# A decoder layer on one Trainium2 core: key loads and table stores in pieces of 32 rows, first phase and rounds resequenced

## Chip, cores and metric

The kernel runs on one core of one Trainium2 chip. The metric is the device time of one execution in microseconds (us). The engines are TensorE (PE), VectorE (DVE), ScalarE (ACT), GpSimd (POOL) and SyncE (SP, which here only issues DMAs).

## What is computed

```python
x = x + swat(layernorm(x))                    # windowed sigmoid attention
x = x + wkv(w, u, k=layernorm(x), v=ctx)      # a recurrence over the 256 rows
x = x + ffn(layernorm(x))                     # ternary weights, 8-bit activations
# swat: 16 heads of 32; K and V are one head of 32 for all
K = rope(x @ wk.T) @ k_compress.T @ k_decompress.T;  V = (x @ wv.T) @ v_compress.T @ v_decompress.T
K, V = quant_dequant_8bit(K), quant_dequant_8bit(V)      # min and max over the whole tensor
for i in range(0, s, 64):                                # windows of 128, step 64
    a = sigmoid(Q[i:i+128] @ K[i:i+128].T * scale);  a = a / (a.sum(-1) + 1e-8)
    out[i:i+128] = blend(out, a @ V[i:i+128])            # linear ramp over the overlap
# ffn, every linear with round(w / mean|w|) in -1, 0, 1 and rows of x on an 8-bit grid
h = silu(x @ gate.T) * (x @ up.T);  h = rms_norm(h) * ln_weight;  x = x + h @ down.T
```

x is 16 batches of 256 rows by 512, float32; gate and up are 2048 x 512, down is 512 x 2048. K and V need the minimum and maximum over all batches, and a weight's grid needs the mean of the whole weight.

## The kernel before

Each engine has a program of its own, written out by hand (`sync_program`, `tensor_program`, `scalar_program`, `vector_program`, `pool_program`); an engine runs its program in order and waits on semaphores (class of events: `x.at(i)` is the count after step i). What runs when is thus set by these five lists and by nothing else. The DMA queue is SP's for nearly all transfers, ACT's for the stores of raw keys and values; a DMA issue also takes its place in the issuing engine's order.

**First phase** (to 78.88 us). For each of 8 pairs of batches, SP loads x (`load_x`, L265) and its transpose (`load_columns`, L271), PE projects keys and values (`keys_project`, L441), spreads the row statistics (L454) and, one pair later, takes the low-rank step (`keys_grow`, L463, L470); DVE makes the statistics, the rope (L917, L924) and the minima and maxima (`keys_ext`); ACT copies the raw keys and values out of PSUM and stores them to DRAM scratch (`keep_raw`, L682 to L690). SP stores, two pairs later still, the cosine and sine rows with the row scaling to the same scratch (`store_trig`, L279). wq is centred with column means from PE (L478) and one pass on DVE (`queries_centre`, L910). DVE sets the grid after an all-reduce on POOL. Of the 12 weight chunks of 1 MB (three weights GATE, UP, DOWN of four chunks) SP loads one at a time into a buffer (`load_weights`, L288), ACT sums the absolute values (`sum_weights`, L698), POOL and DVE make the mean of four chunks (`weight_mean`, L972 to L977), and DVE rounds each chunk (`round_weights`, L936, L939, L945: three passes). The buffer is free for a next chunk when the chunk has been rounded.

**Rounds** i = 0 to 18. Round i has attention of batch b = i, the recurrence of w = i - 1, gate and up of f = i - 2, down of g = i - 3 and the output of h = i - 4. In a round:

- PE: `queries` (L508, two halves), `wkv_keys` (L569, transposes), `gate_up(f, t, k)` (L597; t row half, k column quarter), `scores(b, c)` (L527, four groups of four heads), `down(g, t, k)` (L607), `dens` and `nums` (L538, L541), `wkv_back` (L578), `attention_out` (L559).
- ACT: `set_keys` (L717, L719, L723: the windows of K and V from the loaded rows and the grid), `silu` (L786), `squares` (L791, with the sum of a row), `exps` (L777), `probs` (L734), `logs` and `inverses` (L741, L746), `wkv_logs` and `wkv_inverses` (L752, L757), `scale_tokens` (L764), `scale_hidden` (L770). sigmoid, exp, log and silu change the function table, a row ACT_TABLE_LOAD.
- DVE: `keys_grid` (L1023 to L1029), `blend_windows` (L1051 to L1054), `hidden` (L1160, gate times up), `hidden_scale` (L1176 to L1182), `wkv_residual` (L1110), `wkv_norm` (L1116, L1012), `peak` (L1167, L1169: the sum of the squares and the largest value of the hidden rows), `wkv_quantise` (L1017, L1126 to L1142), `residual` (L1061, L1063), `wkv_round` (L1149), `rope` (L1037), `hidden_round` (L1189), `rotate` (L1043), `values` (L1073), `scan` (L1082), `join` (L1090), `refine` (L1097), `quotient` (L1104), `output` (L1194).
- POOL: `weigh_windows` (L1347), `weigh_hidden` (L1364), statistics (L1324, L1370), `key_steps` (L1354).
- SP: `turn_queries` (L328: neighbouring rows of the rotated queries swapped, two DMAs for each half), `turn_tokens` (L336) and `turn_hidden` (L343), DMA transposes; `load_keys` (L312 keys with cosine and sine, L316 values), `load_queries` (L302), `load_values` (L321), `load_residual` (L297), `store` (L348).

The next queries need the residual rows (`residual`, L1061), which stand on DVE behind `peak` and `wkv_quantise`; `peak(g, 1)` needs the last squares of its half:

```python
            if do_g:
                peak(g, 1)
            if do_f:
                wkv_quantise(f)
            if do_w:
                residual(w)
```

The key load takes 32 rows of 3 x 256 values of a batch's scratch and writes them four times, to partitions 0 to 127; in front of each row lie three windows of the values.

Of the kernel before, what the change touches and what calls it, by code (L numbers as in the profile page):

```python
# [13 lines left out]
P = 128  # L14
# [25 lines left out]
def build(nc, a, out, k_scratch, v_scratch):  # L40
# [118 lines left out]
    v_raw = [raw[k][:, 1] for k in range(4)]  # L159
# [40 lines left out]
    kv_loaded = event("kv_loaded", 2, 16)  # L200
# [11 lines left out]
    key_grown, key_raw, key_ext = event("key_grown", 2), event("key_raw", 2), event("key_ext", 2)  # L212
    w_summed, w_round, w_bound, w_tern = [
# [46 lines left out]
    def sync_program(sy):  # L260
# [30 lines left out]
        def load_residual(b):  # L291
            if b == 0:
                sy.wait_ge(key_bn.sem, key_bn.at(PAIRS - 2))
# [10 lines left out]
        def load_keys(b):  # L304
            if b:
# [59 lines left out]

        for j in range(PAIRS):
# [6 lines left out]
        sy.dma_start(wq_sb[:, :, :], a["wqT"].rearrange("(c p) n -> p c n", p=P)).then_inc(wq_loaded.sem, 16)  # L373
        load_queries(0)
        load_keys(0)
        load_weights(GATE, 0)
        load_weights(GATE, 1)
        store_trig(5)
        load_weights(GATE, 2)
        load_weights(GATE, 3)  # L380
        store_trig(6)
        load_residual(0)
        store_trig(7)
        load_values(0)
        for i in range(B + 3):
# [4 lines left out]
            if do_g:  # L390
                turn_hidden(g, 0, 0)
            if do_b:
                turn_queries(b, 1)
            if do_g:
                turn_hidden(g, 0, 1)
            if i == 0:
                load_weights(UP, 0)
            if i == 1:
                load_weights(DOWN, 1)
            if do_g:  # L400
                turn_hidden(g, 1, 0)
            if do_b:
                next_keys(b)
            if do_g:
                turn_hidden(g, 1, 1)
# [1096 lines left out]
```

## Time and profile before

| | |
|---|---|
| Median of 3 runs | 1096.46 us (1096.4 to 1097.68) |
| The profiled execution: its time | 1100.16 us |
| its span | 1098.8 us |
| mean granted TensorE clock | 0.922 |
| PE busy | 878.8 us, 80% |
| DVE busy | 844.1 us, 77% |
| ACT busy | 706.2 us, 64% |
| POOL busy | 435.7 us, 40% |
| DMA | 106.90 MB, mean 97 GB/s |

Busy times count instructions at work; a wait on a semaphore or for a buffer is idle time. The last column group of a window gives the granted clock, the mean busy share of the 16 DMA engines and what they moved. In a timeline a row groups neighbouring instructions of one line; in brackets stands how long the engine was idle before, and what released it. Rows of SP are DMA issues: their time is that of the issue, not of the transfer. The whole span of 40 slices begins with the DMA at 328 and 314 GB/s for two slices of 27.5 us each and falls to about 80 in the rounds.

### The profile page before, as it was taken

What the parts mean: (1) busy time and instruction counts of PE and PEld (TensorE: products, weight loads), DVE (VectorE), ACT (ScalarE), POOL (GpSimd) and SP (SyncE); (2) the same over time, 40 slices, a digit from 0 to 9 for tenths busy, and PEclk for the clock granted to TensorE, in tenths of its full rate; (3) what the DMA queues carried; (4) which work ended last, traced back from release to release, by engine and by line L of the source; (5) the groups of instructions that cost most, each with busy time, mean ns of one, the idle gap of its engine ahead of it and who ended that gap; (6) DMA issues with size and microseconds to landing.
All of it is one profiled execution on the core that took longest, in us unless ns stands there. A gap on an engine that the chain in (4) does not pass through costs nothing.

```text
span 1098.8 us, 22051 instructions
## 1 busy us (share of the span) xinstructions
PE 878.8 (80%) x8388; PEld 516.9 (47%) x8388; DVE 844.1 (77%) x1630; ACT 706.2 (64%) x1179; POOL 435.7 (40%) x494
## 2 busy tenths in 40 slices
PE   5883656678888888888888888989898888886665
PEld 2342545445454555555545555555455555553222
DVE  4744477887888888888887888888877888876953
ACT  0114737276868686868777777777786868684633
POOL 2100113236263635353535453535454444444522
PEclk9986776869999999999999999999999999997878
DMA  8876424020515151515142524242424343212022
GB/s 328 314 231 246 151 100 148 19 85 10 103 59 103 55 107 54 107 51 99 63 95 67 84 78 84 78 84 79 84 78 72 91 67 95 68 59 40 28 59 67
DMA packets 125754, 106.90 MB, mean 97 GB/s; under 512 B 99312, under 2 KB 101088, under 8 KB 124496
## 3 DMA queue, kind: packets, MB, share of 16 engines
q1 hardware_dynamic: 119344, 101.47, 35.6%
q0 software_dynamic: 624, 2.59, 0.7%
q10 hardware_dynamic: 5680, 1.42, 0.6%
q8 instruction: 66, 1.08, 0.4%
q14 instruction: 40, 0.33, 0.1%
HBM read 65.62 MB, written 10.49 MB: 69 GB/s over the span
## 4 chain that ended last, share of the span: by engine, by line
ACT 30%; PE 26%; DVE 20%; issue 15%; SPq 5%; DMA 2%; POOL 2%; DVEq 0%; ACTq 0%; POOLq 0%
PE bank L508 9%; ACT arena L734 6%; PE bank L607 5%; PE bank L527 4%; ACT L786 3%; ACT sums L741 3%; DVE junk L1160 3%; PE bank L597 3%; ACT sums L746 2%; ACT junk L786 2%; ACT junk L791 2%; DVE amax L1126 2%; DVE fs L1169 2%; ACT L757 2%; ACT L734 2%
## 5 line engine op out<-in xcount | busy, mean ns | idle before, releaser
L597 PE MATMUL bank<-w_up_gate,qT 128*128 128x512 bf16 x1024 | 244.9, 389 | 40.4 <-ACT junk L786 20.6
L1364 POOL TENSOR_TENSOR work<-junk,lnw 128x512 f32<-128x512 f32 x128 | 188.3, 1491 | 126.0 <-DVE junk L1160 111.7
L1347 POOL TENSOR_TENSOR sums<-sums,blend 128x448 f32<-128x448 f32 x64 | 73.6, 1170 | 274.2 <-ACT sums L746 274.2
L597 PEld LDWEIGHTS bank<-w_up_gate,qT 128*128 128x128 bf16 x1024 | 97.2, 100 | 155.8 <-ACT junk L786 26.3
L508 PE MATMUL bank<-wide,wq_sb 128*128 128x256 f32 x512 | 120.8, 397 | 34.8 <-DVE rows L1061 30.8
L607 PE MATMUL bank<-w_down,work 128*128 128x512 bf16 x512 | 132.0, 408 | 19.8 <-ACT junk L786 10.5
L508 PEld LDWEIGHTS bank<-wide,wq_sb 128*128 128x128 f32 x512 | 100.6, 199 | 61.2 <-issue 46.9
L734 ACT ACTIVATE arena<-bank 128x384 f32<-128x384 f32 x256 | 104.9, 497 | 36.0 <-PE bank L527 35.8
L527 PE MATMUL bank<-wide,k_win 32*128 32x128 f32 x1536 | 69.7, 317 | 72.9 <-ACT arena L734 54.2
L786 ACT ACTIVATE junk<-bank,deq 128x512 f32<-128x512 f32 x128 | 86.3, 686 | 54.0 <-PE bank L597 52.2
L559 PE MATMUL bank<-wo_sb,wide 128*128 128x512 f32 x256 | 115.8, 607 | 2.6 <-DVE wide L1054 2.6
L1160 DVE TENSOR_TENSOR junk<-bank,junk 128x512 f32<-128x512 f32 x128 | 87.6, 685 | 29.1 <-PE bank L597 15.8
L527 PEld LDWEIGHTS bank<-wide,k_win 32*128 32x128 f32 x1536 | 56.1, 211 | 97.1 <-ACT arena L734 71.9
L770 ACT ACTIVATE work<-work,fs 128x2048 f32<-128x2048 f32 x32 | 63.9, 1996 | 58.5 <-DVE fs L1182 58.5
L1082 DVE TENSOR_TENSOR_SCAN sums<-wkv_s,sums 128x256 f32<-128x256 f32 x128 | 98.6, 838 | 0.0
L791 ACT ACTIVATE junk<-junk 128x512 f32<-128x512 f32 x128 | 80.7, 630 | 20.7 <-DVE junk L1160 20.6
L607 PEld LDWEIGHTS bank<-w_down,work 128*128 128x128 bf16 x512 | 48.0, 103 | 87.0 <-issue 23.1
L559 PEld LDWEIGHTS bank<-wo_sb,wide 128*128 128x128 f32 x256 | 49.8, 195 | 60.5 <-issue 55.6
L1037 DVE TENSOR_TENSOR wide<-bank,kv_b 128x512 f32<-128x512 f32 x64 | 41.0, 682 | 45.7 <-PE bank L569 38.6
L1169 DVE TENSOR_REDUCE fs<-work 128x1 f32<-128x2048 f32 x32 | 72.8, 2276 | 0.4 <-POOL work L1364 0.4
L764 ACT ACTIVATE wide<-wide,amax 128x512 f32<-128x512 f32 x32 | 21.4, 714 | 79.2 <-DVE amax L1138 79.2
L538 PE MATMUL bank<-arena,v_win 128*32 128x128 f32 x1536 | 57.7, 285 | 9.9 <-ACT sums L741 8.1
(150 smaller groups left out, 1536.9 us busy)
## 6 DMA issues: line engine op xcount, KB each, us to landing
sums<-in_xT SPq DMA_DIRECT2D x8, 1024.0 KB, 11.2
wide<-in_xT SPq DMA_DIRECT2D x16, 512.0 KB, 3.8
rows<-in_x SPq DMA_DIRECT2D x16, 512.0 KB, 4.9
ctx_T<-in_ctxT SPq DMA_DIRECT2D x16, 512.0 KB, 3.7
wide<-wide SPq DMA_DIRECT2D x64, 128.0 KB, 2.0
out<-rows SPq DMA_DIRECT2D x32, 256.0 KB, 2.1
kv_b<-k_raw SPq DMA_DIRECT2D x16, 384.0 KB
work<-in_wgT SPq DMA_DIRECT2D x4, 1024.0 KB, 16.4
```

The lines of the kernel that those rows point to most:

```text
L508: last = te.matmul(in_bank(k, 2)[:, n % 2, :], wq_sb[:, c, n * P:(n + 1) * P], xT[:, c, :], start=c == 0, stop=c == NC - 1)
L527: last = te.matmul(bank[j][:, n * P:(n + 1) * P], k_win[head, window], q_cos[head, c, window], start=True, stop=True, skip_group_check=True)
L559: last = te.matmul(bank[t][:, :], heads_T[:, c, t * P:(t + 1) * P], wo_sb[:, c, :], start=c == 0, stop=c == NC - 1)
L597: last = te.matmul(bank[4 + k % 4][:, :], qT[:, c, t * P:(t + 1) * P], w_up_gate[:, m, c, cols], start=c == 0, stop=c == NC - 1)
L607: last = te.matmul(bank[6 + t][:, :], hid_T[:, t, c, :], w_down[:, c, :], start=c == 0, stop=c == NI - 1)
L734: se.activation(prob[:, :, QUAD * c + j, :], bank[j][:, 0:NW * P].rearrange("p (k q) -> p k q", k=NW), ACT.Sigmoid, scale=float(1.0 / np.s ...
L786: se.activation(gated[:, n % 2, :], bank[4 + 2 * (n % 2)][:, :], ACT.Silu, scale=deq[:, 0, t:t + 1]).then_inc(silu_set.sem, 1)
L791: se.activation(gated[:, n % 2, :], hid[:, n % 2, :], ACT.Square, accum_out=fs[:, t, n:n + 1]).then_inc(sq_set.sem, 1)
L1082: ve.tensor_tensor_scan(state[:, c, n, 1:S + 1], sc["decay"][:, c:c + 1].to_broadcast([P, S]), GG[:, c, n, :], 0.0, ALU.mult, ALU.add).the ...
L1160: ve.tensor_tensor(hid[:, n % 2, :], bank[4 + k % 4][:, :], gated[:, n % 2, :], op=ALU.mult).then_inc(hid_set.sem, 1)
L1169: ve.tensor_reduce(col[t]["am"], hid_w[:, t, :], AX.X, ALU.max, apply_absolute_value=True).then_inc(h_peak.sem, 1)
L1364: ge.tensor_tensor(hid_w[:, t, cols], hid[:, n % 2, :], lnw[:, cols], op=ALU.mult).then_inc(z_set.sem, 1)
```

## The change

- `load_keys` writes the keys in four DMAs of 32 rows in place of one that repeats its source four times; the values come from a scratch laid out as they are used (128 rows of 96 values), for which ACT copies the windows in order before it stores them (three more copies a pair, into space that is free at that time).
- `store_trig` still issues two DMAs, each now of 32 rows by 2 by 256 in place of 2 by 32 by 256.
- wkvT is laid out contiguous and loaded by SP, with low_rank, ahead of everything; SP no longer waits for the two before the second pair; the transpose of x is loaded ahead of x.
- wq and the first queries' rows are loaded after pair 5; wq's means are taken a pair earlier, and its centring stands before the last pair's minima and maxima. ACT issues the loads of the first residual and context.
- Loads, sums and roundings of the weights stand at other places of rounds 0 to 2.
- In every round all five engines' lists are in another order.

```diff
         for j in range(PAIRS):
+            load_columns(j)
             load_x(j)
-            load_columns(j)
-            if j == 0:
-                sy.wait_ge(first_loads.sem, first_loads.at(0))
             if j >= 3:
                 store_trig(j - 3)
...
-            for u in both:
-                sy.dma_start(k_scratch[2 * j + u, :, S:].rearrange("e (n s) -> n e s", n=2),
-                             rope_rows[j][0:2 * HD, u, :]).then_inc(trig_stored[j % 4].sem, 16)
+            for n in both:
+                sy.dma_start(k_scratch[2 * j:2 * j + 2, :, (n + 1) * S:(n + 2) * S].rearrange("u e s -> e u s"),
+                             rope_rows[j][n * HD:(n + 1) * HD]).then_inc(trig_stored[j % 4].sem, 16)
...
-            sy.dma_start(kv_b[:, NW * HD:], k_scratch[b].unsqueeze(0).to_broadcast([QUAD, HD, 3 * S])).then_inc(
-                kv_loaded.sem, 16)
-
-            windows = bass.AP(v_scratch.tensor, v_scratch[b].offset, [[HD, P], [BLK * HD, NW], [1, HD]])
-            sy.dma_start(v_q, windows).then_inc(kv_loaded.sem, 16)
+
+            for k in range(QUAD):
+                sy.dma_start(kv_b[k * HD:(k + 1) * HD, NW * HD:], k_scratch[b]).then_inc(kv_loaded.sem, 16)
+            sy.dma_start(v_q, v_scratch[pair, :, b % 2]).then_inc(kv_loaded.sem, 16)
...
+            new = bank[TOK_BANK[j % 2]][:, 0:4 * 2 * HD].rearrange("p (u t g e) -> p g u t e", u=2, t=NT, g=2)[:, 1]
+            se.copy(v_rows[j % 4][:, :, 0:NW:2, :], new).then_inc(val_rows.sem, 1)
+            se.copy(v_rows[j % 4][0:BLK, :, 1, :], new[BLK:P, :, 0, :]).then_inc(val_rows.sem, 1)
+            se.copy(v_rows[j % 4][BLK:P, :, 1, :], new[0:BLK, :, 1, :]).then_inc(val_rows.sem, 1)
...
-            if j == PAIRS - 1:
+            if j == PAIRS - 2:
                 te.wait_ge(wq_loaded.sem, wq_loaded.at(0))
                 column_means(bank[0][:, :], wq_sb, wq_mean)
...
+            if j == PAIRS - 1:
+                queries_centre()
...
             if do_g:
                 turn_hidden(g, 0, 0)
+                turn_hidden(g, 0, 1)
+                turn_hidden(g, 1, 1)
             if do_b:
                 turn_queries(b, 1)
-            if do_g:
-                turn_hidden(g, 0, 1)
-            if i == 0:
-                load_weights(UP, 0)
+            if i == 0:
+                load_weights(GATE, 3)
...
+            if do_w:
+                values(w)
+                scan(w, 0)
             if i == 2:
                 round_weights(DOWN, 3)
+            if do_b:
+                rotate(b, 1)
```

(The line numbers of the changed kernel are a few higher: L288 is L292 there, L328 is L329, L791 is L795, L1043 is L1048.)

SP's queue from the last table store of the pairs' loop to round 0. Before:

```order
L279 DMA k_raw<-w_down 2x32x256 x2
L373 DMA wq_sb<-in_wqT 128x4x512
L302 DMA wide<-in_xT 128x1024
L312 DMA kv_b<-k_raw 128x1x768
L316 DMA kv_b<-v_raw 128x3x32
L288 DMA work<-in_wgT 128x2048 x2
L279 DMA k_raw<-w_down 2x32x256 x2
L288 DMA work<-in_wgT 128x2048 x2
L279 DMA k_raw<-w_down 2x32x256 x2
L297 DMA rows<-in_x 128x1024
L279 DMA k_raw<-w_down 2x32x256 x2
L321 DMA ctx_T<-in_ctxT 128x1024
L328 DMA wide<-wide 64x512 x4
```

and now:

```order
L283 DMA k_raw<-w_down 32x2x256 x2
L316 DMA kv_b<-k_raw 32x768 x4
L317 DMA kv_b<-v_raw 128x96
L292 DMA work<-in_wgT 128x2048
L283 DMA k_raw<-w_down 32x2x256 x2
L292 DMA work<-in_wgT 128x2048
L283 DMA k_raw<-w_down 32x2x256 x4
L292 DMA work<-in_wgT 128x2048
L329 DMA wide<-wide 64x512 x4
L292 DMA work<-in_wgT 128x2048
L292 DMA work<-in_wuT 128x2048 x2
```

The swaps (L328, now L329) stood behind four GATE chunks, the residual's and the context's loads; now three chunks are ahead of them and the fourth is behind.

ACT at the boundary of two full rounds, from the last silu of one round to the exps of the next (fs is the sum of squares and the scales, v_win and k_win are what `set_keys` writes). Before:

```order
L786 ACTIVATE junk<-bank,deq 128x512
L791 ACTIVATE junk,fs<-junk 128x512 x2
L770 ACTIVATE work<-work,fs 128x2048
L764 ACTIVATE wide<-wide,amax 128x512 x2
L717 ACTIVATE v_win<-kv_b,grid 128x96
L719 ACTIVATE v_win<-kv_b,grid 64x32
L723 ACTIVATE k_win<-kv_b,grid 128x256
L770 ACTIVATE work<-work,fs 128x2048
L786 ACTIVATE junk<-bank,deq 128x512
L777 ACT_TABLE_LOAD
L777 ACTIVATE sums<-bank,wkv_s 128x256 x4
```

and now:

```order
L795 ACTIVATE junk,fs<-junk 128x512
L721 ACTIVATE v_win<-kv_b,grid 128x96
L723 ACTIVATE v_win<-kv_b,grid 64x32
L727 ACTIVATE k_win<-kv_b,grid 128x256
L795 ACTIVATE junk,fs<-junk 128x512
L774 ACTIVATE work<-work,fs 128x2048
L768 ACTIVATE wide<-wide,amax 128x512 x2
L774 ACTIVATE work<-work,fs 128x2048
L790 ACTIVATE junk<-bank,deq 128x512
L795 ACTIVATE junk,fs<-junk 128x512
L790 ACTIVATE junk<-bank,deq 128x512
L781 ACT_TABLE_LOAD
```

`set_keys` has moved from behind `scale_tokens` to ahead of the last squares, and the first squares and a second silu stand ahead of the exps.

## Rows read from the trace of the kernel before

**Rows 1.** Windows: us, busy us (instructions) by engine, TensorE clock, DMA share, GB/s
```profile
0.00:78.88 78.88, 59.19 (x197) 27.46 (x197) 43.96 (x127) 9.15 (x19) 12.75 (x25) 0.97 0.87 295
78.88:141.77 62.89, 35.68 (x400) 26.36 (x401) 30.97 (x53) 34.30 (x48) 6.65 (x8) 0.68 0.54 184
141.77:204.18 62.41, 34.42 (x417) 26.26 (x417) 46.38 (x81) 30.93 (x50) 13.57 (x14) 0.73 0.33 109
...
323.65:379.33 55.68, 48.37 (x512) 28.96 (x513) 46.90 (x92) 42.05 (x72) 26.07 (x29) 1.00 0.35 80
```

**Rows 2.** Waits of SP, 10 to 111 us
```profile
SPq L265 <- DMA arena<-in_low_rank: 9.5, 1, 9.5
```

**Rows 3.** SP timeline, first phase: start, duration, what [idle before, releaser]
```profile
66.20 6.71 SPq L279 DMA_DIRECT2D k_raw<-w_down  x2
...
92.44 2.48 SPq L328 DMA_DIRECT2D wide<-wide  x4
```

**Rows 4.** Timeline of PE, first phase and first scores
```profile
26.88 3.63 PE L441 MATMUL bank<-sums,arena 128*96 128x512 f32 x8
...
32.78 3.63 PE L441 MATMUL bank<-sums,arena 128*96 128x512 f32 x8
...
63.00 3.67 PE L441 MATMUL bank<-sums,arena 128*96 128x512 f32 x8 [1.09 <-DMA sums<-in_xT]
...
78.88 10.14 PE L508 MATMUL bank<-wide,wq_sb 128*128 128x256 f32 x32 [3.96 <-DVE wq_sb L910]
102.00 1.67 PE L527 MATMUL bank<-wide,k_win 32*128 32x128 f32 x24 [12.97 <-DVE wide L1043]
```

**Rows 5.** The chain that ended last, 78 to 105 us
```profile
93.00 8.13 DMA wide<-wide
```

**Rows 6.** The page's DMA issues: count, KB each, median us to landing
```profile
wide<-wide SPq DMA_DIRECT2D x64, 128.0 KB, 2.0
```

**Rows 7.** Timeline of ACT, end of round 0
```profile
130.62 1.91 ACT L698 ACTIVATE junk<-work 128x2048 f32<-128x2048 f32 x1
```

**Rows 8.** Timeline of DVE, end of round 0
```profile
136.83 0.15 DVE L974 TENSOR_SCALAR w_mean<-abs_tot 128x1 f32<-128x1 f32 x1 [4.02 <-POOL abs_tot L1328]
...
140.94 0.68 DVE L1061 TENSOR_TENSOR rows<-bank,rows 128x512 f32<-128x512 f32 x1
```

**Rows 9.** Two windows of the first phase (columns as above)
```profile
15.00:40.00 25.00, 25.00 (x81) 10.91 (x80) 22.11 (x66) 3.14 (x8) 6.07 (x10) 1.00 1.02 391
41.70:43.70 2.00, 2.00 (x9) 0.64 (x7) 0.74 (x2) 0.00 (x0) 0.00 (x0) 1.00 0.54 91
```

**Rows 10.** Timeline of ACT, a full round
```profile
342.19 1.64 ACT L734 ACTIVATE arena<-bank 128x384 f32<-128x384 f32 x4
...
371.66 0.63 ACT L791 ACTIVATE junk<-junk 128x512 f32<-128x512 f32 x1 [0.28 <-DVE junk L1160]
...
379.59 0.45 ACT L717 ACTIVATE v_win<-kv_b,grid 128x96 f32<-128x96 f32 x1
...
380.50 0.60 ACT L723 ACTIVATE k_win<-kv_b,grid 128x256 f32<-128x256 f32 x1
```

**Rows 11.** Timeline of DVE, the same round
```profile
373.03 0.12 DVE L1167 TENSOR_REDUCE fs<-fs 128x1 f32<-128x4 f32 x1
```

**Rows 12.** Timeline of SP's queue, the same round
```profile
335.95 1.10 SPq L328 DMA_DIRECT2D wide<-wide  x2
337.15 2.62 SPq L343 DMA_TRANSPOSE work<-work  x2
339.94 0.58 SPq L312 DMA_DIRECT2D kv_b<-k_raw  x1
```

**Rows 13.** Timeline of PE, the same round, and of the drain
```profile
323.65 7.14 PE L508 MATMUL bank<-wide,wq_sb 128*128 128x256 f32 x32 [1.64 <-DVE rows L1061]
...
346.59 0.95 PE L527 MATMUL bank<-wide,k_win 32*128 32x128 f32 x24
...
1032.98 4.86 PE L597 MATMUL bank<-w_up_gate,qT 128*128 128x512 bf16 x12 [2.82 <-DVE rows L1194]
```

More of the change, by code:

```diff
@@ L158, in build @@
     raw = [small(P, 2 * 2 * NT * HD).rearrange("p (g n e) -> p g n e", g=2, n=2 * NT) for k in range(4)]
-    v_raw = [raw[k][:, 1] for k in range(4)]
+    v_rows = [home[:, n * 2 * NW * HD:(n + 1) * 2 * NW * HD].rearrange("p (u k e) -> p u k e", u=2, k=NW) for home in
+              (q_tok[:, :, :].rearrange("p t d -> p (t d)").bitcast(fp32), qT[:, :, :].rearrange("p c s -> p (c s)").bitcast(fp32))
+              for n in both]
     wkv_sb = small(P, NC * 3 * HD).rearrange("p (c n) -> p c n", c=NC)
@@ L409, in sync_program @@
             if i == 0:
-                load_weights(UP, 1)
+                load_weights(UP, 3)
+            if do_w:
+                next_values(w)
+            if do_g:
+                store(g, 1)
+            if do_w:
+                next_residual(w)
+            if i == 1:
+                load_weights(DOWN, 3)
             if i == 1:
@@ L619, in tensor_program @@
                 queries(b, 1)
+            if do_f:
+                gate_up(f, 0, 0)
             if do_w:
@@ L801, in scalar_program @@
                 set_keys(b)
+            if i == 0:
+                sum_weights(GATE, 2)
+            if do_g:
+                squares(g, 1, 3)
+                scale_hidden(g, 0)
+            if do_f:
+                scale_tokens(f)
             if do_g:
@@ L805, in scalar_program @@
                 silu(f, 0, 0)
+                squares(f, 0, 0)
+                silu(f, 0, 1)
             if do_w:
@@ L808, in scalar_program @@
             if do_f:
-                silu(f, 0, 1)
-                squares(f, 0, 0)
+                squares(f, 0, 1)
+                silu(f, 0, 2)
+                silu(f, 0, 3)
+            if i == 1:
+                sum_weights(DOWN, 0)
+            if do_b:
+                probs(b, 0)
             if i == 0:
                 sum_weights(GATE, 3)
-            if do_f:
-                silu(f, 0, 2)
-                squares(f, 0, 1)
-                silu(f, 0, 3)
             if do_b:
-                probs(b, 0)
+                probs(b, 1)
+            if i == 1:
+                sum_weights(DOWN, 1)
             if do_f:
@@ L821, in scalar_program @@
             if do_b:
-                probs(b, 1)
                 probs(b, 2)
@@ L849, in scalar_program @@
             if do_b:
-                logs(b, 2)
-                logs(b, 3)
                 inverses(b, 2)
                 inverses(b, 3)
+            if do_f:
+                silu(f, 1, 0)
             if i == 1:
                 sum_weights(DOWN, 2)
-            if do_f:
-                silu(f, 1, 0)
-                silu(f, 1, 1)
+            if i == 1:
+                sum_weights(DOWN, 3)
             if i == 0:
@@ L861, in scalar_program @@
             if do_f:
+                silu(f, 1, 1)
                 squares(f, 1, 0)
@@ L864, in scalar_program @@
                 squares(f, 1, 1)
+                silu(f, 1, 3)
+                squares(f, 1, 2)
             if i == 0:
                 sum_weights(UP, 3)
-            if i == 1:
-                sum_weights(DOWN, 3)
-            if do_f:
-                silu(f, 1, 3)
-                squares(f, 1, 2)
-                squares(f, 1, 3)
-                scale_hidden(f, 0)
-            if do_w:
-                scale_tokens(w)
-            if i == 0:
-                sum_weights(DOWN, 0)
     def vector_program(ve):
@@ L1259, in vector_program @@
             if do_g:
-                hidden_scale(g, 1)
+                hidden_round(g, 0)
+            if do_f:
+                hidden(f, 0, 0)
             if do_b:
```

175 lines of the change are left out of this document (74 added, 101 removed).

## The prediction

> **What bounds the kernel now.** I read the sum by rounds first. The span falls into a first phase of 78.88 us, three filling rounds, of which the first two take 62.89 and 62.41 us at a granted clock of 0.68 and 0.73, thirteen full rounds of which one of 55.68 us stands here, and a drain [rows 1]. In a full round TensorE (PE) is busy 48.37 of 55.68 us and VectorE (DVE) 46.90, so neither is the bound by itself: what sets a round is a loop of hand-overs. The first round is where time lies idle: PE works 35.68 of 62.89 us.
>
> Then the first phase, on SyncE (SP), the DMA queue on which nearly everything is issued. SP does not pass its second pair of loads until low_rank has landed, a wait of 9.5 us [rows 2]. Later its issues stretch: one pair of table stores takes 6.71 us to issue, four swaps 2.48 [rows 3]. PE goes from pair to pair in 5.90 us while it is fed (26.88, 32.78), but from 32.78 to 63.00 it needs 30.2 us for four pairs, and then stands 3.96 us for the centring of wq before the queries at 78.88 [rows 4]. The first scores start at 102.00 after 12.97 us idle, and the chain says why: the swap of the rotated halves, issued at 92.44 behind the weights and the context, needs 8.13 us to land [rows 4, 5], where the median swap takes 2.0 us [rows 6]. After that the round ends with a chain of weights: the last sum on ScalarE (ACT) from 130.62 (to 132.6 with its read-out), the all-reduce and mean at 136.83, the rounding of an UP chunk in three passes, and only then, at 140.94, the residual [rows 7, 8].
>
> **First phase, start.** wkvT contiguous and low_rank alone at the head of the queue: SP was let go at 11.2 before, when low_rank had landed beside the first loads of x. A transfer of this kernel that has the engines to itself lands in about 2 us (the median swap, 128 KB, [rows 6]); I take some 4 us for the two loads at the start, so the pairs start 7 us earlier. Bounds: 0 (the 16 MB of x come first anyway) and 9.5, the whole wait.
>
> **First phase, pace.** Two table stores a pair keep their number and bytes, but their rows (32, not 2) are outermost. The trace has one look at such a store with little beside it: 41.70 to 43.70 shows a DMA share of 0.54 at 91 GB/s, against 1.02 at 391 GB/s while loads run alone [rows 9]. At 391 GB/s the 2 MB of a pair take 5.4 us, less than PE's 5.90. So I let the pairs run at PE's pace: 4 x 5.90 = 23.6 in place of 30.2, a gain of 6.6. Bounds: 0 (the loads go on sharing engines with stores) and 6.6. The centring moves one pair ahead: 4.0 of wait goes. Three more ACT copies a pair lie beside PE's 5.90. 78.88 - 7 - 6.6 - 4.0 = 61.3. Against this: 17.5 MB at 391 GB/s are 45 us that must land before the end; I allow 2.7 us for it. **Queries at 64 instead of 78.88.**
>
> The Trainium skill, page "DMA: Bandwidth & Descriptors", section "Why a DMA increments its semaphore by 16 and not by 1", says that a transfer is spread over as many engines as divide its outermost dimension on both sides, at most 16: by it a store with 2 outermost runs on two engines and one with 32 on all. That agrees with the low share and rate of the window above. By it the sum would keep my 6.6; without it the stall is only the amount of data, and the pace gains nothing. The same page's "Rules for kernel authors" speaks against the other half of the change: two transfers to disjoint sets of partitions serialise, and one is better. By it the four loads of 32 rows gain nothing.
>
> **The key load in four pieces.** In my sum it gains and costs nothing as well, for a reason of the trace: a full round issues it at 339.94 [rows 12] and its first reader, the grid on DVE, runs behind the reduction of the first half, some 14 us later. SP has three more issues of some 0.5 us, and is idle most of a round. Bounds: 0 and 3 x 0.58 = 1.7 us of SP, hidden by those 14 us.
>
> **First round.** The queries run at full clock, 7.14 us and not 10.14 [rows 4, 13]: 64 to 71. Swap 0 follows without weights ahead of it: 1.1 us of issue, 2.0 of landing, an addition of 0.7: scores at about 75, 27 us earlier. Now the cost: the load of GATE 3 stands behind both swaps. It lands at 80 (1 MB in some 5 us), is summed by 82, mean by 83; four roundings of 3.8 us end at 98.5. UP 3 and UP 2 can only be loaded then (their buffers come free), 2 MB at some 300 GB/s: 106. Two sums of 1.9 end at 110; from the last sum to the end of the first UP rounding it took 140.94 - 132.6 = 8.3 [rows 7, 8]: 118.5. **Queries 1 at 119 in place of 141.77: -23.** So 27 won at the scores, 4 given back on the weights. Bounds: -28, if the weights' chain is hidden, and -12 (start and centring alone, pace and swap half).
>
> **Rounds 1 and 2.** The sum of DOWN 1 (1.9 us) stands between two probs on ACT, and the later sums push silu: +1.7; round 2 +0.3. Bounds 0 and +4.
>
> **Full rounds.** Two pieces lengthen the loop. (a) silu 0, the product, its squares and silu 1 are before the exps now; before, the exps followed silu 0 directly. silu 1 waits for the second gate product, queued behind the wkv transposes on PE. By the old durations probs 0 start at 342.5 instead of 342.19 [rows 10]: +0.3. (b) set_keys ran at the round's end behind scale_tokens, where nobody waited (379.59 to 381.1, three activations, 1.5 us together). Now it is ahead of the last squares (371.66 before) [rows 10]. DVE's reduction at 373.03 waits for those squares, and through it the norm, the quantisation and residual that release the next queries [rows 11]. The squares' read-out ended at 372.39, 0.64 ahead of the reduction; 1.5 less that slack is +0.9 at most; set_keys can start as soon as squares 2 have ended (371.39), 0.28 ahead: +0.6. Sum +0.9 a round, x 13 = **+11.3**. Bounds: 0 (DVE is late anyway) and +1.9.
>
> In the order of DVE, rotate 1 now stands behind half the scan; it would be done at 343.9, and its reader, the third scores, starts at 346.59 [rows 13]: 2.7 us of cover, nothing in the sum. The output of g moves from behind the join to behind the next peak: its store and the load of xT behind it come at about 357, needed at 379. Cover 15 us.
>
> **Drain.** PE stood 2.82 us at 1032.98 for an output before gate_up [rows 13]; the back products no longer queue behind that, and the join ends 1.3 us earlier. -2.3; bounds 0 and -4.
>
> **Sum:** -23 + 2.0 + 11.3 - 2.3 = -12.0. The profiled execution took 1100.16 us, 3.7 above the median of 1096.46; off the median that is **1084.5**, off the profiled one 1088.
>
> **Rivals.** *Rounds as long as before* (chance 0.25): -23 + 2 - 2.3 = -23.3, 1073. For it: DVE is busy 46.90 of 55.68 us and may come late to the reduction by itself; against: only 0.64 us of slack at the reduction. *The first phase gives half* (0.15): the loads stay the bound, or the UP loads come late, -12; with the rest -1: 1095. *A late second swap* (0.08), the one on the slower side: swap 1 is now issued behind three transposes, 1.3 us of issue each (two take 2.62, [rows 12]), on the same queue. Before, it was issued at 335.95 with one ahead of it (same rows); I reckon its landing at 342.8, just when DVE comes to rotate 1. If it needs what the first swap needed (8.13 and not 2.0), it lands 6.1 us later, 3.4 beyond the cover; 13 x 3.4 = 44, and the time is 1128. From 3.8 us late on (1.1 us a round) the kernel is slower than before. Against it: the transposes move 0.25 MB each and no weights or x are in the queue then. *The change does not do what it says* (0.04): the four loads bring the same bytes to the same rows, and the stores' shape is hidden; only the resequencing remains; no time apart from those above, about 1090.
>
> **How the numbers follow.** My forecast has 0.48, the rivals 0.25, 0.15, 0.08 and 0.04. The range takes in the rounds unchanged (1073, less 2 for the first phase) and the half gain (1095, and 1 more): 1071 to 1096. A measurement here can tell 0.2%, 2.2 us, from nothing. Faster needs under 1094.3: 0.48 + 0.25 + 0.04 + a third of 0.15, 0.82. Within: 0.07. Slower: 0.08 and the rest of the half gain, 0.11.
>
> **What would show it.** Right: queries 0 at 64 at clock 1.0, scores 0 near 75, queries 1 near 119, a swap of 2 us in round 0; full rounds of 56.6 with DVE idle before its fs reduction for squares. Wrong: key projections still over 7 us apart; queries 1 later than 130; rounds at 55.7 or under; DVE idle before rotate 1 for the swap.

## The result and the profile after

| | before | after |
|---|---|---|
| median of 20 runs each | 1097.2 us (1092.8 to 1100.8) | 1106.5 us (1100.7 to 1110.0) |
| ratio | | 1.0079, 95% interval 1.0064 to 1.0094 |
| the profiled execution, span | 1098.8 us | 1106.0 us |
| mean granted clock | 0.922 | 0.903 |
| queries of round 0, 1, 2, 3 start at | 78.9, 141.8, 204.2, 266.9 | 73.3, 125.7, 189.1, 253.5 |
| an undisturbed full round | 55.7 us | 58.0 us |
| last queries start; from there to the end | 942.4; 156.4 | 952.0; 154.0 |

The kernel became slower by 0.8%, where the prediction had it faster by 1.1%, and 1106.5 lies above its range. The windows of the changed kernel, columns as in [rows 1], put the gain and the loss in their places:

```profile
0.00:73.27 73.27, 60.11 (x197) 28.03 (x197) 42.57 (x121) 12.86 (x39) 12.39 (x24) 0.95 0.89 331
73.27:125.72 52.45, 33.77 (x403) 24.74 (x402) 32.53 (x57) 36.69 (x55) 8.70 (x9) 0.74 0.59 207
125.72:189.09 63.37, 34.16 (x418) 26.13 (x417) 46.14 (x81) 31.16 (x50) 12.21 (x14) 0.74 0.32 108
...
371.50:429.61 58.11, 49.63 (x513) 30.56 (x513) 47.60 (x92) 42.17 (x72) 25.75 (x29) 0.94 0.33 77
```

At the queries of round 1 the changed kernel is 16.05 us ahead (forecast 23). Rounds 1 and 2 cost 0.96 and 1.61 more (forecast 2.0 together). From the queries of round 3 to the last, twelve rounds, it takes 698.5 us in place of 675.5: 23.0 lost, where the forecast had 11.3 over thirteen. The end gives 2.3 back, as forecast. Together +7.2 us of span. So the sign turns on the full rounds, and there on what follows. In the kernel before seven of these twelve rounds take 55.7 to 55.8 us and five take 56.7 to 58.4, the mean is 56.3; in the changed kernel the mean is 58.2.

PE's timeline of a full round that starts at 371.50, the counterpart of [rows 13]:

```profile
371.50 7.14 PE L512 MATMUL bank<-wide,wq_sb 128*128 128x256 f32 x32 [2.19 <-DVE rows L1066]
...
386.35 0.95 PE L531 MATMUL bank<-wide,k_win 32*128 32x128 f32 x24
389.04 1.90 PE L611 MATMUL bank<-w_down,work 128*128 128x512 bf16 x8 [1.74 <-ACT junk L790]
391.99 0.95 PE L531 MATMUL bank<-wide,k_win 32*128 32x128 f32 x24 [1.05 <-ACT arena L738]
394.64 1.67 PE L531 MATMUL bank<-wide,k_win 32*128 32x128 f32 x24 [1.71 <-ACT arena L738]
398.02 1.67 PE L531 MATMUL bank<-wide,k_win 32*128 32x128 f32 x24 [1.71 <-ACT arena L738]
399.62 2.77 PE L611 MATMUL bank<-w_down,work 128*128 128x512 bf16 x8
```

The scores of groups 2 and 3 (from 394.64 and 398.02) take 1.67 us, those of 0 and 1 take 0.95, as all four did in the round of before; the product behind them takes 2.77, not 1.90. All thirteen full rounds of the changed kernel are like that (groups 2 and 3 take 1.48 to 1.67 us). Four windows of the same round, columns as in [rows 1], say what that is:

```profile
391.00:393.00 2.00, 0.95 (x24) 0.76 (x24) 0.57 (x1) 0.98 (x4) 0.00 (x0) 1.00 0.94 238
395.00:397.00 2.00, 1.31 (x24) 1.01 (x20) 2.00 (x2) 0.87 (x4) 1.68 (x2) 0.50 0.17 43
397.00:399.00 2.00, 0.98 (x16) 0.98 (x20) 2.00 (x5) 1.57 (x5) 0.00 (x0) 0.50 0.00 0
403.00:405.00 2.00, 2.00 (x96) 2.00 (x91) 1.53 (x5) 1.87 (x4) 0.00 (x0) 1.00 0.03 8
```

The granted clock is 1.00 at 391 and 0.50 from 395 on, so the array runs at 1.2 GHz and not 2.4, and is back at 403. Between 386 and 395 PE had two groups of scores of 0.95 us, one down product of 1.90, and waits of 1.74, 1.05 and 1.71. Before, some of those waits were filled: gate_up 3 stood behind scores 0, and down(g,0,1) between scores 1 and 2. PE of the kernel before, in the round from 323.65:

```profile
338.27 1.90 PE L597 MATMUL bank<-w_up_gate,qT 128*128 128x512 bf16 x8 [0.54 <-ACT junk L786]
340.93 1.90 PE L607 MATMUL bank<-w_down,work 128*128 128x512 bf16 x8 [0.76 <-ACT junk L786]
343.88 0.95 PE L527 MATMUL bank<-wide,k_win 32*128 32x128 f32 x24 [1.05 <-ACT arena L734]
344.76 1.90 PE L607 MATMUL bank<-w_down,work 128*128 128x512 bf16 x8
```

The slow clock adds 2 x 0.72 + 0.87 = 2.3 us to PE's work, and since ACT's probs wait for the scores, most of it is on the chain. Set against each round's own queries (371.50 and 323.65), the steps of the chain lie as follows:

| step, us after the queries' start | before | after | lost |
|---|---|---|---|
| probs 0 start on ACT | 18.54 | 18.79 | 0.25 |
| probs 1 | 21.19 | 21.45 | 0.26 |
| probs 2 | 23.91 | 24.83 | 0.92 |
| probs 3 | 26.56 | 28.20 | 1.64 |
| silu of the second half | 41.25 | 43.14 | 1.89 |
| sum of squares reduced on DVE (L1167, now L1172) | 49.38 | 51.77 | 2.39 |
| next queries | 55.68 | 58.11 | 2.43 |

The first two lines are my term (a), 0.3. Then 1.38 us are lost at the two slow groups and 0.25 behind the slow down product: none of this was in the sum. The step before the reduction is the 0.5 that I put on set_keys. ACT of the same round, the probs and the two lines on the disputed step:

```profile
390.29 1.64 ACT L738 ACTIVATE arena<-bank 128x384 f32<-128x384 f32 x4
...
399.70 1.64 ACT L738 ACTIVATE arena<-bank 128x384 f32<-128x384 f32 x4 [1.13 <-PE bank L531]
...
421.11 0.45 ACT L721 ACTIVATE v_win<-kv_b,grid 128x96 f32<-128x96 f32 x1
...
422.53 0.61 ACT L795 ACTIVATE junk<-junk 128x512 f32<-128x512 f32 x1
```

DVE and POOL of the same round: the second swap, the reduction, and what POOL ends just ahead of it:

```profile
392.43 0.69 DVE L1048 TENSOR_TENSOR wide<-wide 128x512 f32<-128x512 f32 x1 [2.74 <-DMA wide<-wide]
...
423.27 0.16 DVE L1172 TENSOR_REDUCE fs<-fs 128x1 f32<-128x4 f32 x1
```

```profile
417.22 0.88 POOL L1373 TENSOR_TENSOR fs<-fs,minus_half 128x1 f32<-128x1 f32 x1
...
418.32 4.97 POOL L1363 TENSOR_TENSOR work<-junk,lnw 128x512 f32<-128x512 f32 x4
```

set_keys does hold the last squares: they start at 422.53, 1.3 us after the ones before them have ended, and not 0.28. But POOL too is late: it multiplies the hidden rows until 423.29, and the reduction behind it (L1174) needs those. It had lost time in two small steps of the statistics, 0.37 us (from 416.77) and 0.88 (417.22), which before took 0.19 and 0.59. The second swap kept DVE waiting 2.74 us; its addition ended at 393.1, before scores 2 at 394.64, and DVE stands 3.70 us for POOL later in the round (until 408.30): a wait, and covered, as reckoned.

### The profile page after: what moved, and what is told of

Read it like the earlier page. It is cut to its first block, busy times and chain, and to the rows that moved or that the text cites. A ratio compares the mean times of both kernels' runs of the same rounds, so it can differ in the third digit from the quotient of the medians.

```text
span 1106.0 us, 22123 instructions
## 1 busy us (share of the span) xinstructions
PE 881.0 (80%) x8388; PEld 533.6 (48%) x8388; DVE 854.0 (77%) x1630; ACT 712.2 (64%) x1203; POOL 431.7 (39%) x494
## 4 chain that ended last, share of the span: by engine, by line
ACT 35%; PE 29%; issue 13%; DVE 13%; POOL 3%; DMA 2%; SPq 0%; DVEq 0%; ACTq 0%; POOLq 0%
PE bank L512 11%; ACT arena L738 8%; PE bank L531 6%; PE bank L601 5%; ACT junk L790 3%; ACT sums L745 3%; ACT L790 3%; ACT junk L795 3%; ACT sums L750 2%; ACT L750 2%; PE bank L611 2%; DVE amax L1131 2%; ACT L781 2%; ACT L745 2%; ACT sums L781 2%
## 5 line engine op out<-in xcount | busy, mean ns | idle before, releaser
L601 PE MATMUL bank<-w_up_gate,qT 128*128 128x512 bf16 x1024 | 238.4, 384 | 27.1 <-DMA qT<-q_tok 22.0
L1363 POOL TENSOR_TENSOR work<-junk,lnw 128x512 f32<-128x512 f32 x128 | 168.6, 1337 | 185.1 <-DVE junk L1165 166.6
L1346 POOL TENSOR_TENSOR sums<-sums,blend 128x448 f32<-128x448 f32 x64 | 76.9, 1213 | 235.9 <-ACT sums L750 223.4
L531 PE MATMUL bank<-wide,k_win 32*128 32x128 f32 x1536 | 87.0, 376 | 89.4 <-ACT arena L738 80.2
L512 PE MATMUL bank<-wide,wq_sb 128*128 128x256 f32 x512 | 118.0, 390 | 36.2 <-DVE rows L1066 36.2
L531 PEld LDWEIGHTS bank<-wide,k_win 32*128 32x128 f32 x1536 | 71.1, 263 | 111.2 <-ACT arena L738 95.4
L795 ACT ACTIVATE junk<-junk 128x512 f32<-128x512 f32 x128 | 81.2, 634 | 36.4 <-DVE junk L1165 36.4
L1087 DVE TENSOR_TENSOR_SCAN sums<-wkv_s,sums 128x256 f32<-128x256 f32 x128 | 103.2, 864 | 0.0
L1174 DVE TENSOR_REDUCE fs<-work 128x1 f32<-128x2048 f32 x32 | 72.8, 2275 | 0.9 <-POOL work L1363 0.9
L1056 DVE TENSOR_TENSOR wide<-bank,sums 128x64 f32<-128x64 f32 x64 | 13.9, 217 | 69.2 <-POOL sums L1346 69.1
```

The source lines that it names most:

```text
L512: last = te.matmul(in_bank(k, 2)[:, n % 2, :], wq_sb[:, c, n * P:(n + 1) * P], xT[:, c, :], start=c == 0, stop=c == NC - 1)
L531: last = te.matmul(bank[j][:, n * P:(n + 1) * P], k_win[head, window], q_cos[head, c, window], start=True, stop=True, skip_group_check=True)
L601: last = te.matmul(bank[4 + k % 4][:, :], qT[:, c, t * P:(t + 1) * P], w_up_gate[:, m, c, cols], start=c == 0, stop=c == NC - 1)
L795: se.activation(gated[:, n % 2, :], hid[:, n % 2, :], ACT.Square, accum_out=fs[:, t, n:n + 1]).then_inc(sq_set.sem, 1)
L1087: ve.tensor_tensor_scan(state[:, c, n, 1:S + 1], sc["decay"][:, c:c + 1].to_broadcast([P, S]), GG[:, c, n, :], 0.0, ALU.mult, ALU.add).the ...
L1346: ge.tensor_tensor(soft[:, c, :], soft[:, c, :], blend[:, :], op=ALU.mult).then_inc(weighted.sem, 1)
```

## The experiments

All times are medians; the kernel before ran beside each.

**Put the down product back between the scores** (changed kernel).

```diff
             if do_b:
                 scores(b, 1)
+            if do_g:
+                down(g, 0, 1)
+            if do_b:
                 scores(b, 2)
                 scores(b, 3)
-            if do_g:
-                down(g, 0, 1)
```

> The changed kernel, with one PE step put back: down(g,0,1) between the second and third scores, where it stood before. Clock theory: its 1.9 us of dense products keep the granted clock at 1.0 there, scores 2 and 3 take 0.95 us and not 1.67, the down product 1.9 and not 2.77; a full round falls by about 1.6 (from 58.1 to 56.5), the kernel by 13 x 1.6 = 21, to about 1085. Rival (traffic): the scores are slow because the second swap, the transposes and the key loads land beside them; then the clock or the duration stays as it is, the round stays at 58.1 and the time at 1106.

Measured: 1102.9 us (before 1096.6), ratio 1.0064 (1.0047 to 1.0081). Some PE rows of it, the last from the next round:

```profile
308.22 8.83 PE L512 MATMUL bank<-wide,wq_sb 128*128 128x256 f32 x32 [2.18 <-DVE rows L1067]
...
327.44 1.90 PE L611 MATMUL bank<-w_down,work 128*128 128x512 bf16 x8 [1.73 <-ACT junk L791]
330.39 0.95 PE L531 MATMUL bank<-wide,k_win 32*128 32x128 f32 x24 [1.05 <-ACT arena L739]
...
333.10 0.95 PE L531 MATMUL bank<-wide,k_win 32*128 32x128 f32 x24
335.76 1.53 PE L531 MATMUL bank<-wide,k_win 32*128 32x128 f32 x24 [1.71 <-ACT arena L739]
...
366.95 7.15 PE L512 MATMUL bank<-wide,wq_sb 128*128 128x256 f32 x32 [2.18 <-DVE rows L1067]
```

Scores 2 run at 0.95 us, so what stands between the scores decides their speed: the traffic is the same. But only two full rounds take 56.5 us. The clock still falls in every full round, now as late as scores 3 (1.53 us) or behind them, and in most rounds a second time at the queries: in 10 of 13 they take about 8.8 us instead of 7.14, after 2.18 us of idle, where the changed kernel has the same idle and 8.83 in one. The fall had moved, and of 21 us only 3.6 came back by the medians, 1.6 by the ratios, whose intervals overlap.

**The opposite edit in the kernel before**: down(g,0,1) behind scores 3.

> The kernel before, with one step moved: down(g,0,1) behind the fourth scores, so that scores 1, 2 and 3 stand side by side. Clock theory: the granted clock falls to half there as in the changed kernel, scores 3 (and perhaps 2) take 1.67 us, a full round grows from 55.7 by 0.7 to 1.6 us, the kernel to 1106 to 1118. Rival (traffic): DMA and DVE are as before, the scores stay at 0.95 us; the round loses nothing, the time stays at 1097 or falls a little.

Measured: 1140.9 us, ratio 1.040. PE in a full round:

```profile
347.02 0.95 PE L527 MATMUL bank<-wide,k_win 32*128 32x128 f32 x24 [1.71 <-ACT arena L733]
349.68 1.66 PE L527 MATMUL bank<-wide,k_win 32*128 32x128 f32 x24 [1.71 <-ACT arena L733]
351.28 4.32 PE L607 MATMUL bank<-w_down,work 128*128 128x512 bf16 x16
355.53 0.86 PE L538 MATMUL bank<-arena,one_win 128*32 128x128 f32 x24
```

The fourth group takes 1.66 us; in other rounds the third does too, and rounds take 58.2 to 60.8. One product of 1.9 us moved by two places, with nothing else touched, costs 44 us: more than I gave the clock theory. Not all of it is the clock. The moved product now stands ahead of `dens`, which start 31.4 us after the queries (355.53 - 324.14) and not 28.3 (351.96 - 323.65); 1.4 of these 3.1 us are slow work (0.71 on scores 3, 0.69 on the two products), the rest is the product's new place, and some 0.7 of it was slack, since before ACT came to its logs 0.8 us after `dens` 0 had ended. That leaves an estimate of 1 us a round, some 13 of the 44, for the order alone, and some 30 for the clock; my expectation that the order alone loses nothing was wrong. Stores, loads, and DVE's and ACT's lists are those of before, so traffic as the cause of the slow scores is out.

**set_keys back behind scale_tokens** (changed kernel).

> The changed kernel, with set_keys on ACT put back behind the scaling of the tokens, so that the last squares are not held by it. By the trace of the changed kernel the last squares start 1.05 us too late and the reduction on DVE 0.50 us: a full round falls by 0.5, the kernel by 13 x 0.5 = 6.5, to about 1100. Rival: DVE or POOL is late by itself and only 0.1 is gained, 1105.

Measured: 1105.4 us (ratio 1.0077 against the same kernel before; the changed kernel had 1.0079). The round stays at 58.0. DVE's reduction and the next queries:

```profile
418.19 2.29 DVE L1174 TENSOR_REDUCE fs<-work 128x1 f32<-128x2048 f32 x1 [0.17 <-POOL work L1363]
```

```profile
424.47 7.14 PE L512 MATMUL bank<-wide,wq_sb 128*128 128x256 f32 x32 [2.20 <-DVE rows L1066]
```

The reduction now waits for POOL's products, and PE idles 2.20 us as before the edit. The ordering that I had priced at 0.6 a round costs nothing that can be seen: behind it stood the prediction's rival that DVE "may come late to the reduction by itself", with POOL as its partner.

**Both put back.**

> The changed kernel with both steps put back, down(g,0,1) between scores and set_keys behind the scaling. If the two terms are independent: 1106 - 21 - 6.5 = about 1079, full rounds of 56.0 us. If one covers the other: 1085.

Measured: 1105.0 us, ratio 1.0072. Three rounds take 56.5; in ten of 13 the queries run at half clock. The terms were not independent, and neither of my numbers came.

**The start alone, with the rounds of before**: rounds 0 and 1 in the new order, all five lists from round 2 on in the old.

```diff
-        for i in range(B + 3):
+        for i in range(2):
...
+        for i in range(2, B + 3):
```

(the second loop has the body of before, without the weights done already; ACT scales the tokens of batch 0 between the two.)

> First phase and rounds 0 and 1 of the changed kernel, rounds 2 to 18 in the order of before on all five engines (the four-piece key load and the new scratches stay). Theory: the start is worth the 16 us that the changed trace shows at the queries of round 1, and the rounds go back to 55.7 us with a granted clock of 1.0: 1096.5 - 16 = 1080. Rival (the key load in four pieces or the new value load costs in every round): the rounds stay above 57, the time above 1095. Rival (the chip takes the clock back in any order after a denser start): time between 1085 and 1095, rounds with queries of 8.8 us.

Measured: 1083.3 us, ratio 0.988 (0.986 to 0.990). Queries 1 at 123.8, rounds of 55.7 to 58.4 as in the kernel before. So the start's gain is real, and the loss is in the order of the lists from round 2 on (1106.5 against 1083.3 us; by the ratios some 22 us); the key load in pieces costs nothing there.

**PE's list alone in the order of before** (changed kernel, from round 2).

> The changed kernel with PE's list alone in the order of before from round 2 on (gate_up 3 between scores 0 and the first down product, wkv transposes first, dense products spread between the scores and behind them). Clock theory: scores and down run at full speed, a full round is 56.5 us or below; if the queries too keep the clock, the time is 1106 - 21 = 1085; if the clock falls at other idle places, as in the run with down alone put back, 1100 to 1103. Rival (traffic): no change, 1106.

Measured: 1128.1 us, ratio 1.029. Rounds of 58.2 to 61.4. The clock is not the whole of that: the round from 432.22 has its queries at 7.14 and all four scores at 0.95 us and still takes 59.2. An order of PE on its own is not good or bad: against the changed lists of ACT and DVE it waits in new places, in that round 2.35 us for the rotated queries ahead of scores 0. My expectation took PE's list out of its company.

**The table stores' shape alone** (kernel before).

```diff
-            for u in both:
-                sy.dma_start(k_scratch[2 * j + u, :, S:].rearrange("e (n s) -> n e s", n=2),
-                             rope_rows[j][0:2 * HD, u, :]).then_inc(trig_stored[j % 4].sem, 16)
+            for n in both:
+                sy.dma_start(k_scratch[2 * j:2 * j + 2, :, (n + 1) * S:(n + 2) * S].rearrange("u e s -> e u s"),
+                             rope_rows[j][n * HD:(n + 1) * HD]).then_inc(trig_stored[j % 4].sem, 16)
```

> The kernel before with the table stores alone in their new shape (32 rows outermost). If the shape holds the queue, SP's issues of them fall from 2.5 to 6.7 us to 0.8, the loads come earlier and queries 0 start several us before 78.88 (I expect 3 to 6), the time falls to 1091 to 1094. Rival: the amount of data is the bound, nothing moves, 1096.5.

Measured: 1083.4 us, ratio 0.988 (0.986 to 0.990). SP, and PE's last pair and queries 0:

```profile
25.26 0.82 SPq L279 DMA_DIRECT2D k_raw<-w_down  x2
```

```profile
55.02 3.62 PE L441 MATMUL bank<-sums,arena 128*96 128x512 f32 x8
...
70.56 9.37 PE L508 MATMUL bank<-wide,wq_sb 128*128 128x256 f32 x32 [3.97 <-DVE wq_sb L910]
```

Beside the loads of the pairs the issue of two stores takes 0.8 to 0.9 us, where it took 1.2 to 3.0; of the one behind the first weights 1.94, where it took 6.71 [rows 3]. The pairs run at PE's pace (the last starts at 55.02, not 63.00), and queries 1 start at 125.4, where the whole resequenced start has 125.7. Such a start is read from one profile each: in the six kernels with the changed start and the changed rounds 0 and 1 it lies between 123.5 and 127.5. The times say the same, though: 0.988 here and 0.988 for the whole new start with the rounds of before. Two changed lines are worth as much as the entire new start.

**The key load in pieces alone** (kernel before).

> The kernel before with the key load alone in four DMAs of 32 rows. My prediction said nothing is gained or lost: 1096.5, within 2 us. Rival: the three more issues delay the transposes behind them on SP, the hidden products are late and the time rises by up to 13 x 1 us.

Measured: 1092.3 us, ratio 0.9959 (0.9942 to 0.9975). PE of the start:

```profile
79.50 9.98 PE L508 MATMUL bank<-wide,wq_sb 128*128 128x256 f32 x32 [3.96 <-DVE wq_sb L910]
96.17 1.67 PE L527 MATMUL bank<-wide,k_win 32*128 32x128 f32 x24 [6.70 <-DVE wide L1043]
```

The queries do not move, but the first scores start at 96.2 and not 102.0: behind the key load in SP's queue the table stores and weights go faster (the stores at 65.05 take 3.85 us where they took 6.71), so swap 0 is issued 2.9 us earlier and waits less. Queries 1 start 6.0 us earlier.

**Both of these together** (kernel before).

> The kernel before with two parts of the change and nothing else: the table stores 32 rows outermost and the key load in four pieces. Alone they gave 1083.4 and 1092.3 against 1096.7. If each takes away a hold of the queue of its own they add up: 1096.7 - 13.3 - 4.4 = 1079. Rival (one queue, one bound: the second gives nothing once the first is gone, or the sum, mean and rounding of the UP weights then end last in round 0): 1082 to 1084. Either would beat both kernels.

Measured: 1081.8 us, ratio 0.985 (0.983 to 0.988): better than both kernels, and by the ratios some 3 us better than the stores alone (0.988). The product of the two single ratios is 0.984, inside the interval, and the interval of the stores alone (0.986 to 0.990) overlaps it too: whether the two parts add up or partly overlap can't be told. The queries of round 1:

```profile
123.54 7.14 PE L508 MATMUL bank<-wide,wq_sb 128*128 128x256 f32 x32
```

No wait stands before them: PE goes there directly from attention_out, which had waited 3.68 us for the windows of round 0. The chain that ended last there runs through the load of an UP chunk (issued at 87.07, 8.04 us), its sum on ACT and the probs behind that: the weights bound round 0 now, and no longer the hold of the stores.

**Three steps put back** (changed kernel: down between the scores, exps directly behind the first silu, on POOL the statistics ahead of the third window).

> The changed kernel with three steps of a round altered: down(g,0,1) between scores 1 and 2; on ACT the exps directly behind the first silu as before; on POOL the statistics of the first half ahead of the third window, so that they do not hold the hidden products. The trace puts 1.64, 0.25 and about 0.35 us on these in a round at full clock: 58.1 - 2.2 = 55.9. Clock theory: PE then stands under 1.9 us before the queries, they keep 7.14 us, and the time is 1106 - 13 x 2.2 = 1077 or a little above. Rival (the clock falls once a round whatever the order is): rounds of 57 to 58.4 with queries of 8.8 us, 1095 to 1103.

Measured: 1118.2 us, ratio 1.018: both times are wrong. The clock did what I hoped for, the queries keep 7.14 us after 2.09 us of idle in 10 of 13 rounds, and such rounds still take 58.3. DVE in a full round:

```profile
389.02 0.69 DVE L1166 TENSOR_TENSOR junk<-bank,junk 128x512 f32<-128x512 f32 x1 [2.57 <-issue]
```

DVE's list still has the second product of the hidden rows ahead of the second rope. With the exps first, silu 1 is 1.3 + 1.6 + 1.3 us later, DVE stands 2.57 us for it, and the rope, the rotation and the first scores stand behind that. The exps could be late only because DVE's order had been made for it.

**The new start with the old stores** (changed kernel, stores 2 outermost).

> The changed kernel with the table stores in their old shape (2 outermost). If the shape is what the first phase gained by, its queries of round 1 go back from 125.7 to about 141, and the time rises by 13 to 16 us, to about 1120. Rival (the resequencing, with the transposes first, the loads of weights behind the swaps and no wait for low_rank, carries the gain by itself): it stays within 5 us of 1106.

Measured: 1113.8 us, ratio 1.0157 where the changed kernel has 1.0079. Queries 1 at 133.1. Between the two expectations: with the stores held, the new sequence keeps 8.6 us of its 16 over the kernel before at the queries of round 1 (good to some 2 us, as above); the key pieces alone gave 6.0 there.

**The down product and POOL's statistics** (changed kernel).

> The changed kernel with down(g,0,1) between scores 1 and 2 and, on POOL, the statistics of the first half ahead of the third window; ACT's list stays. The first step alone gave rounds of 56.5 at full clock, but queries of 8.83 us after 2.18 us of idle in most rounds, 58.3. If POOL's work was what held DVE's reduction by 0.2 to 0.4 us, the round at full clock is 56.1 to 56.3 and PE stands 1.8 to 2.0 before the queries. Clock theory: if that brings the idle near the 1.64 of the kernel before, the queries keep 7.14 in most rounds and the time falls to about 1080; if 1.8 to 2.0 is still too long, rounds stay at 58, 1100 to 1103.

Measured: 1107.1 us, ratio 1.0088 (1.0059 to 1.0118), no gain. Rounds whose queries keep the clock take 57.3, not 56.2. DVE and POOL at the place of the edit:

```profile
411.86 1.25 DVE L1060 TENSOR_TENSOR wide<-sums 128x192 f32<-128x192 f32 x1
```

```profile
411.63 1.26 POOL L1364 TENSOR_TENSOR work<-junk,lnw 128x512 f32<-128x512 f32 x1
```

An addition on DVE that takes 0.36 us (as at 367.00 before) takes 1.25 when POOL begins a product of 1.26 us beside it, and the quotient that PE's back products wait for comes late. POOL was moved out of one collision into another. That the 0.5 us of the changed kernel is such a collision fits its rows (POOL's small steps above; DVE's addition at 413.33 takes 0.96 us, at 365.17 before 0.47), but no run isolates it. The Trainium skill, page "SBUF — State Buffer", section "SBUF: two separate sides", says that VectorE, when both its inputs lie in SBUF, and a GpSimd operation that reads SBUF contend for a shared port pair, which the one that starts first holds for its whole instruction. The rows agree: POOL's product runs from 411.63 to 412.89, and the addition, begun at 411.86, ends only at 413.11.

**Only the idle before the queries lengthened** (kernel before; the statistics of 128 rows are written a second time with the same values).

```diff
                 wkv_quantise(f)
+                ve.bn_stats(stats["wkv"][0][:, 1, :], x_rows[f % 3][:, 1, :])
             if do_w:
                 residual(w)
```

> The kernel before with one vector instruction of 0.6 us doubled (statistics of 128 rows, written again with the same values) right ahead of the residual, so that PE stands about 2.25 us before each queries instead of 1.64. Plain cost: 0.6 a round, 1097 + 9 = 1106. Clock theory: the idle is long enough for the clock to fall, the first queries take 8.83 in most rounds, a round costs 2.3 more, 1120 to 1127. If the queries stay at 7.14, idle before the queries alone does not decide it.

Measured: 1120.2 us, ratio 1.0215. One vector instruction of 0.6 us costs 24 us, of which 13 x 0.6 = 8 are its own time. PE of one round:

```profile
441.92 8.68 PE L508 MATMUL bank<-wide,wq_sb 128*128 128x256 f32 x32 [2.49 <-DVE rows L1061]
```

Idle 2.2 us in place of 1.64, the queries then take 8.7 to 8.8 us in 10 of 13 rounds; one round whose queries keep the clock is 56.3, 0.6 more than before, as plain arithmetic has it.

## Why the prediction was wrong

- **The bound, and the first phase: right in kind, too large.** -16 and not -23. The stores' shape was the cause of the holds, as the run with the stores alone shows; the pace of 5.90 came. The window that I took it from [rows 9] was thin evidence: a share of 0.54 of 16 engines is more than the two engines that I matched it with. What failed is the allowance of 2.7 us for the amount of data: pair 6, the last but one, waited for its statistics until 55.54, PE idle 2.82 (DVE had stood 5.14 us for its rows of x, until 51.16), and at half clock the means of wq took 5.79 us and not 3.70. Queries 0 came at 73.3, not 64. PE's rows and SP's issues there:

```profile
49.09 3.63 PE L443 MATMUL bank<-sums,arena 128*96 128x512 f32 x8
55.54 0.64 PE L456 MATMUL bank<-ident,rstd_x 128*96 128x128 f32 x4 [2.82 <-POOL rstd_x L1323]
...
59.19 5.79 PE L482 MATMUL bank<-wq_sb,arena 128*128 128x512 f32 x8
64.83 3.60 PE L443 MATMUL bank<-sums,arena 128*96 128x512 f32 x8
...
73.27 7.12 PE L512 MATMUL bank<-wide,wq_sb 128*128 128x256 f32 x32
83.94 1.66 PE L531 MATMUL bank<-wide,k_win 32*128 32x128 f32 x24 [3.54 <-DVE wide L1048]
```

```profile
27.07 0.80 SPq L283 DMA_DIRECT2D k_raw<-w_down  x2
...
61.77 8.61 SPq L283 DMA_DIRECT2D k_raw<-w_down  x4
...
80.47 2.45 SPq L329 DMA_DIRECT2D wide<-wide  x4
```

  The store before the swaps still took 8.61 us for four, behind the pair's loads and the weights; the swaps were issued as the queries ended and landed in about 2 us. First scores at 83.9 (75 forecast), and from there 41.8 us to queries 1 where I reckoned 44. "Start 7 us earlier" came for PE's first product (4.17, not 11.36) and was gone by pair 2, which starts at 25.45, and at 25.47 with the stores alone: the pairs waited for x.
- **The key load in pieces: half right.** Hidden in the rounds, as said. But it was also on the start's queue, which I did not cost, and there it gave 4.4 us alone. I weighed the rule that disjoint pieces serialise, and passed over the one beside it. The Trainium skill, page "DMA: Bandwidth & Descriptors", section "Rules for kernel authors", says that a leading broadcast of c copies confines a transfer to at most c engines, so the old load to four. By the one rule 0, by the other a gain; the run has the gain, though no row shows on how many engines a transfer ran.
- **Rounds 1 and 2, the drain: right** (+2.6 for +2.0; -2.3 for -2.3).
- **Full rounds: the step that failed.** "Two pieces lengthen the loop" put +0.9 on a round; it was +2.43 in the round shown (58.11 for 55.68) and +1.9 in the mean of twelve. Term (a) was right, 0.25 for 0.3. Term (b) came to 0.5 for 0.6 by size, but not from set_keys, as the run with it put back showed; POOL and DVE getting into each other's way is the likely cause. The third piece, 1.4 + 0.25, was missing: I read PE's new order of scores 1, 2, 3 and took their durations from the trace of before, at a clock that the old order had kept up. The prediction gives the move of the down product no term at all; of PE it says only that it isn't "the bound by itself". The run with the new start and the rounds of before gives the price of the order as a whole, 22 to 23 us; the two runs that moved this one product by itself show that it sets the speed of the scores behind it.
- **The rivals.** The late swap came, as DVE's wait of 2.74, which I had named as a sign of being wrong, but inside the cover, so it cost nothing. My case for slower had the right sign and the wrong mechanism. I had the numbers to see the right one: the granted clock of 0.68 in a round with idle [rows 1] and queries of 10.14 after 3.96 us of idle [rows 4] stood in my own rows.

What stays open: why after 2.18 us of idle the queries keep the clock in 12 of 13 rounds of the changed kernel and lose it in 10 of 13 when the down product is put back. The idle just before is not all that decides. Nor is it whether the clock had fallen earlier in the round: it falls at or behind the scores in every full round of both. No run isolates what does. Nor does any run bring the changed rounds to a steady clock, so what they would take then is known only from single rounds: 56.5 us with the down product put back, still 0.8 more than before.

## What to carry to other kernels

A filler on TensorE that gates nothing can still be worth more than two per cent (some 30 of 1097 us above, an estimate): when products are moved out of the gaps between small ones, cost every small one at half clock as well, and look at the granted clock in windows of 1 to 2 us before and behind the place. Try the parts of a change one at a time: here two lines on a store's shape gave 13 us, and the reordering of the rounds took away more than 20. Lists of several engines are tuned to each other, so a step put back in one of them alone tells little.

## What the runs showed of the hardware

- The clock fell from 1.00 to 0.50 with no idle stretch above 1.74 us since the queries; just before, TensorE had done 0.95, 1.90 and 0.95 us of work between waits of 1.74, 1.05 and 1.71.
- In the kernel before, the queries after 1.63 to 1.76 us of idle kept 7.14 us in all 12 rounds, those after 1.91 took 8.83; with 2.2 us in the same kernel they lost 1.7 us in 10 of 13. That is no threshold: with stores and pieces together the queries after 1.91 kept 7.14, with three steps put back they did after 2.09 in 10 of 13, and in the changed kernel after 2.17 to 2.30 in 12 of 13.
- Two DMA stores with 2 outermost took 1.2 to 3.0 us to issue beside the loads of the pairs, and 6.71 behind the first weights, and held all behind them [rows 3]; with 32 outermost, the same bytes, 0.8 to 0.9 and 1.94; but four of them took 8.61 at 61.77 in the changed kernel.
- A VectorE addition of 0.36 us took 1.25 beside a GpSimd product.
